# A wait ahead of the loads that add x onto minus x: they begin only once the row of t has landed

## The reference, cut to what matters

```python
HW = h @ W
s = HW @ a[:OUT_F, 0]
t = HW @ a[OUT_F:, 0]
e = jax.nn.leaky_relu(s[row] + t[col], negative_slope=ALPHA)
m = jax.ops.segment_max(e, row, num_segments=N_NODES)
ex = jnp.exp(e - m[row])
den = jax.ops.segment_sum(ex, row, num_segments=N_NODES)
att = ex / den[row]
agg = jax.ops.segment_sum(att[:, None] * h[col], row, num_segments=N_NODES)
...
out = jax.nn.silu(agg) @ base_w.T + jnp.einsum('nip,oip->no', basis, spline_w)
...
x = _layernorm(x + out, axis=-1)
```

## Time and profile before

| | us |
|---|---|
| median of three runs | 389.68 |
| lowest and highest run | 388.93 and 390.03 |
| profiled execution, its own time | 388.39 |
| span of the profiled execution, first to last instruction | 386.6 |
| PE busy | 370.7 (96%) |
| DVE busy | 336.4 (87%) |
| ACT busy | 255.9 (66%) |
| POOL busy | 37.0 (10%) |

### The profile page before, as it was taken

How to read it: one execution, slowest core, us unless ns; L and a number is a source line. 1 busy time by engine, 2 the same in 40 slices (tenths; PEclk the granted TensorE clock), 3 DMA queues, 4 the chain that set the end, 5 groups by cost and what they waited for, 6 DMA issues and landing times.

```text
span 386.6 us, 5456 instructions
## 1 busy us (share of the span) xinstructions
PE 370.7 (96%) x2082; PEld 305.7 (79%) x2082; DVE 336.4 (87%) x430; ACT 255.9 (66%) x256; POOL 37.0 (10%) x92
## 2 busy tenths in 40 slices
PE   6896979999999999999999999999999999999994
PEld 3676658888888888888888888888888888888883
DVE  8997699987775789999899998988999799999445
ACT  6799454545446979774887774897667697776122
POOL 6002201000000010100101010100100101011000
PEclk9999899999999999999999999999999999999998
DMA  7918905100000047477554646442333353564202
GB/s 252 397 22 138 253 13 163 57 2 0 2 0 0 3 140 241 159 203 232 173 185 122 193 120 189 139 109 56 110 114 103 91 142 121 152 196 100 65 29 109
DMA packets 23980, 47.30 MB, mean 122 GB/s; under 512 B 1936, under 2 KB 2412, under 8 KB 23954
## 3 DMA queue, kind: packets, MB, share of 16 engines
q0 software_dynamic: 12416, 24.00, 24.2%
q1 hardware_dynamic: 11538, 22.95, 17.8%
HBM read 44.37 MB, written 2.57 MB: 121 GB/s over the span
## 4 chain that ended last, share of the span: by engine, by line
PE 86%; DVE 5%; DMA 4%; issue 2%; POOL 1%; ACT 1%; SPq 1%; DVEq 0%; POOLq 0%
PE PS L1449 38%; PE PS L1445 25%; PE PS L1384 18%; PE PS L1364 3%; DMA gentle<-t_row 2%; DMA t_row<-strow 1%; PE PS L1394 1%; DVE oh L574 1%; DVE still L590 1%; DVE oh L540 1%; PE PS L1459 0%; SPq L410 0%; PE PS L1325 0%; DVE hit L553 0%; DVE pat L563 0%
## 5 line engine op out<-in xcount | busy, mean ns | idle before, releaser
L1449 PE MATMUL PS<-wh,s 128*128 128x512 f32 x432 | 139.4, 390 | 0.0
L1449 PEld LDWEIGHTS PS<-wh,s 128*128 128x128 f32 x432 | 81.2, 188 | 16.8
L1445 PE MATMUL PS<-s,wh 128*128 128x482 f32 x288 | 92.8, 383 | 0.0
L1449 PE MATMUL PS<-wl,s 128*128 128x512 f32 x216 | 84.2, 390 | 0.0
L1162 ACT ACTIVATE s<-v 128x1220 fp32r<-128x1220 f32 (+1 forms) x32 | 40.0, 1250 | 37.5 <-DVE v L952 26.3
L1445 PEld LDWEIGHTS PS<-s,wh 128*128 128x128 f32 x288 | 54.6, 189 | 9.7
L1145 ACT ACTIVATE v<-xt,bias 128x1220 f32<-128x1220 f32 (+1 forms) x32 | 42.9, 1342 | 20.0 <-DVE s L962 18.0
L1445 PE MATMUL PS<-s,wl 128*128 128x482 f32 x144 | 55.2, 384 | 0.0
L946 DVE SCALAR_TENSOR_TENSOR v<-v,v 128x1220 f32<-128x1220 f32 (+1 forms) x32 | 46.4, 1450 | 7.1 <-ACT v L1148 7.1
L952 DVE SCALAR_TENSOR_TENSOR v<-v,v 128x1220 f32<-128x1220 f32 (+1 forms) x32 | 46.8, 1461 | 3.3
L962 DVE SCALAR_TENSOR_TENSOR s<-v,s 128x1220 fp32r<-128x1220 f32 (+1 forms) x32 | 46.4, 1454 | 1.3 <-ACT s L1162 1.3
(11 more groups left out here) (164 smaller groups left out, 429.7 us busy)
## 6 DMA issues: line engine op xcount, KB each, us to landing
wh<-in_splT POOLq DMA_DIRECT2D x32, 512.0 KB, 4.2
wring<-in_splT SPq DMA_DIRECT2D x21, 512.0 KB, 4.5
xt<-in_xT SPq DMA_DIRECT2D x1, 2500.0 KB, 12.0
xh<-in_x POOLq DMA_DIRECT2D x1, 2304.0 KB, 12.0
wh<-in_baseT POOLq DMA_DIRECT2D x4, 512.0 KB, 5.4
out<-xr SPq DMA_DIRECT2D x8, 256.0 KB
wring<-in_baseT SPq DMA_DIRECT2D x3, 512.0 KB, 3.9
xr<-in_x SPq DMA_DIRECT2D x1, 1280.0 KB, 6.4
```

The costliest lines, as they stand in the source:

```text
L1445: m = e.matmul(PS[:, w, 0:TURNED], wx[:, ic, 128 * w:128 * w + 128], sx[:, ic, 0:TURNED], start=begins, stop=ends_)
L1449: m = e.matmul(PS[:, out_bank(w), :], sx[:, ic, c:c + 128], wx[:, ic, :], start=begins, stop=ends_)
```

## The change

One line is added to POOL's program, ahead of the loop that issues the loads that add x onto xl. Nothing is taken away, and no other engine's program changes.

```diff
+            e.wait_ge(s_trow, 16)
             for part, (lo, hi) in enumerate(zip(ADDED, ADDED[1:] + (NT - 1,))):
                 e.wait_ge(s_neg, NT if hi == NT - 1 else hi)
                 e.dma_start(xl[:, lo:hi, :], x[128 * lo:128 * hi, :].rearrange("(w p) i -> p w i", p=128), accum_op=ALU.add
```

## The result

| | before | after |
|---|---|---|
| median of the runs on one chip, us | 389.36 (388.93 to 390.03, 4 runs) | 385.79 (385.65 to 386.03, 4 runs) |
| profiled execution, us | 388.39 | 386.03 |
| its span, us | 386.6 | 384.1 |

The ratio is 0.9915, interval 0.9898 to 0.9931: faster by 0.7 to 1.0%, 3.6 us by the medians and 2.4 us by the two profiled executions. The sign and the first half of the mechanism were right. A second gain, which I had put at a chance of 0.06, came with it; and the constant by which I went from the profiled execution to the median did not hold.

A forecast was written before the change was run, and what follows sets the result against it. PE carries 86% of the chain, but its start waits for the row, held up by additive loads. Profiled execution: 388.39 - 1.7 (earlier weights) + 0.1 (wait for xl) = 386.8; median 389.68 - 1.6 = 388.1 us, range 387.2 to 390.2.

The forecast's parts named there:

- the first half of the mechanism: Start of tile 0's weights: additive loads hold up the row; holding them back brings the weights 1.7 us forward.
- A second gain: Counting stage: it also ends earlier, for instance if DVE's 2.16 us of "issue" were a held-up fetch; chance 0.06.
- What holds up the row: Writes of t_row and load of trow: additive loads delay both; without them trow lands at 37.8 instead of 44.81.
- Rival (2): Writes of t_row slow by themselves: trow still issued at 36.8, xl lands at 58.2, 391.5 us, slower; chance 0.10.
- What ends the wait then: Before tile 0's weights: ACT's last counts, ending at 44.65, become late; line 774 begins at 45.0, gaining 1.7 us.
- When xl lands: POOL's four additive loads, issued behind trow: all land 17.0 us after it, at 54.8 instead of 49.97.
- The rule against: POOL's issues beside DVE's one-hot operands: each could lose up to 1.21 us, xl at 56.0 to 57.2, 389.3 to 390.5 us.
- When TensorE wants xl: Tile 0's products by xl: the fifth, which needs the last three pieces, is wanted at 54.7 instead of 56.4.
- the 0.1 us of wait: PE ahead of the fifth product by xl: xl at 54.8, wanted at 54.7, costs 0.1 us.
- The profile against the median: Whole-kernel time: the profiled execution's 386.8 us was carried over to a median of 388.1 us.
- rival (3): Row at 36.9 or before and counting ends earlier too: up to 2.5 us gained, 387.2 us; chance 0.06.
- the same difference put on the median: Whole-kernel time: profiled execution before was 1.3 us below the median, so 389.68 - 1.6 = 388.1 us.

The follow-up runs named there:

- e3_stall_back: The kernel after, with DVE's 2.2 us stall in the counting stage put back by two unused reductions; 386.32 us, profiled execution 386.48.
- e1_writes: The kernel after, but the additive loads wait only until the four writes of t_row have landed, not for trow; 385.01 us.
- e9: The kernel before, unchanged, run again for a second profiled execution; 388.96 us.
- e10: The kernel before, unchanged, run once more for a third profiled execution; 389.30 us.
- e5_plain: The kernel before with its additive loads made plain at the same places, sizes and times (low part of x wrong); 384.50 us.
- e4_row_behind: The kernel after, but loads wait only for the writes of t_row, and SP holds the row's load until TensorE turned s; 390.75 us.

## Why the prediction was wrong, point by point

- **What holds up the row: right.** The writes land at 32.69 (forecast 33.4), trow at 37.08 (37.8). Rival (2), writes slow by themselves, is out: 1.59 us from the last issue. The sentence of the Trainium skill on late completions in device memory ("DMA: Bandwidth & Descriptors", section "Anatomy of one DMA — SWDGE (gpsimd) path") did not decide here: the target was the same in both kernels, and what lay beside the writes made the difference between 5.70 and 1.59 us.
- **What ends the wait then: right in kind, wrong in time.** The counts release the marks, but at 42.39. This is the first of the two steps that failed. I took ACT's end at 44.65 from the earlier trace rows as fixed, although DVE's 2.16 us of "issue" stood in the row that I quoted. I named a held-up fetch as its possible cause, called it unexplained and gave it 0.06. The row of line 302 would have settled it before: DVE's program has a load of registers just there, and the trace of before has its 4542 ns. e3_stall_back shows the size of what was left out: with the stall in place the forecast for the profiled execution, 386.8, holds within 0.3 us.
- **When xl lands: right.** Trow at 37.08 plus 17.0 gives 54.1; the wait ended at 54.07. The rule against, that of the Trainium skill on descriptors ("SBUF — State Buffer", section "SBUF: two separate sides"), did not show: in e1_writes POOL's issue at 34.81 ran beside DVE's one-hot operands and took the 1.29 us that it took before beside an idle DVE. In the kernel after the second issue took 1.87 us, but it began at 38.18, while the first (1.35 us from 37.37) still ran.
- **When TensorE wants xl: wrong by the same step.** 2.3 us earlier counts make the 0.1 us of wait 1.8. Of the 2.3 us by which the counts end earlier, the wait leaves 0.45 (386.48 - 386.03, the profiled executions of e3_stall_back and the kernel after).
- **The profile against the median: wrong, and the larger part of the miss.** For the profiled execution I forecast 386.8, and 386.03 came, 0.8 below; for the median 388.1, and 385.79 came, 2.3 below. The other 1.5 us lie in "the same difference put on the median", the second step that failed. I added the 1.3 us by which the median of before lay above its profiled execution, and the median of the kernel after lies 0.2 below its own. This constant is also what puts the time outside the range: rival (3), which has the second gain, allowed 2.5 us, which is 385.9 for the profiled execution and fits, and ended at 387.2 only through it. In part the 1.3 us was contention on the row, which the change removes (0.75 and 0.90 us at line 774 in e9 and e10), and in part the few runs behind the median: it was 389.68 in three runs, 389.36 in four, and 388.84 in seventeen of another set. How much falls to each stays open.

In sum, on the profiled execution: row 1.7, stall 2.3, wait for xl -1.8, together 2.2 (measured 2.4). By the medians of the result 1.2 more: the median of before lies 1.0 above its profiled execution, that of the kernel after 0.2 below.

## What to carry to other kernels

Before costing a wait as the next one that is late, ask whether that wait's own cause is touched by the change as well: every stretch of "issue" in the window deserves a name, and register loads have rows under the line of their helper. A large transfer that nobody needs soon should be issued behind the small ones that many wait for: queued behind them, xl came 1.8 us too late; queued ahead, it made the weights of tile 0 start 4.1 us later. Before carrying a difference from a profiled execution over to the median, ask whether the change removes what makes the two differ, and count the runs behind the median. And when a transfer then comes late by a microsecond, look for products of the same tile that don't need it before shortening the transfer.

## What the runs showed of the hardware that I had not expected

- A load of five registers from SBUF takes 1.41 to 1.47 us, alone or beside plain loads at 407 GB/s, and 4.54 to 4.88 us beside loads that add onto SBUF. The Trainium skill ("Runtime: NRT & Kernel Launch", section "Instruction fetch mechanics") states some 200 ns a register for loads from HBM, the device memory; no run here loads registers from there. These, from SBUF, take 0.28 us each, as a mean of the five, where they are not disturbed and 0.91 where they are.
- The adding loads run at some 200 to 210 GB/s where they have the DMA engines to themselves, and these are counted as over-full (a share of 1.10 to 1.15); the plain ones run at about twice that (407 GB/s in e5_plain).
- A queue can get nothing while another is served. In e1_writes POOL's queue moved nothing in 34 to 38 us while SP's row was on its way; before, SP's moved nothing in 38 to 40 us. But what was there first does not always go first to its end: in e4_row_behind the row, issued at 37.03, got nothing until 41 us and then shared with POOL's loads, 88 packets against 87 in 42 to 44 us. What makes the one or the other happen is not shown.

```profile
q1 hardware_dynamic: 88, 0.45, 59.5%
q0 software_dynamic: 87, 0.18, 47.6%
```
